# A four-stage Mamba, attention and experts model on one core: the experts' rounds written as one block, and decays, z, statistics and setup of the Mamba stage moved

## The reference, cut to what matters

```python
# step 1: four Mamba layers on x; per layer
xin, z = split(einsum('bld,ed->ble', layernorm(residual), in_w))   # 2 x 256 channels
u  = silu(causal_conv(xin, cw) + cb)                               # 4 taps
dtr, B, C = split(u @ xp_w.T)                                      # 8, 16, 16
dt = softplus(dtr @ dtp_w.T + dtp_b)
for n in range(16):                                                # states
    h[n] = exp(dt * A[n]) * h[n] + dt * u * B[n]                   # scan over the tokens
y  = (sum_n h[n] * C[n] + u * D) * silu(z)
hidden = y @ out_w.T
# step 2: cross-attention, 16 heads      step 3: experts (below)
# step 4: trajectory attention           step 5: top-k self-attention, cross-attention, ffn
# step 6: ternary-quantised gated ffn
# step 3: 8 heads choose 1 of 2048 experts each by product keys; their rows are gathered
lin = (x . A_in[idx]) * relu(score);  hid = gelu(x @ W_in.T + lin . B_in[idx])
out = hid @ W_out.T + ((hid . A_out[idx]) * gate) . B_out[idx]
```

## Time and profile before

| | us |
|---|---|
| median of 3 runs (lowest, highest) | 7854.28 (7828.51, 7878.61) |
| profiled execution, its span | 7862.71, 7860.9 |
| setup | 0 to 118 |
| Mamba stage | 118 to 3761 |
| cross-attention | 3761 to 4498 |
| experts | 4498 to 5514 |
| trajectory | 5514 to 5822 |
| decoder | 5822 to 7535 |
| last ffn | 7535 to 7861 |

### The profile page before, as it was taken

One profiled execution on the slowest core, in us unless ns is written; L12 is line 12 of the kernel. 1 busy time (PEld: TensorE's weight loads), 2 busy tenths in 40 slices (PEclk: granted clock), 3 DMA queues, 4 the chain that ended last, 5 costly groups with the idle time before them and its releaser, 6 DMA issues. The chain is left out here.

```text
span 7860.9 us, 92400 instructions
## 1 busy us (share of the span) xinstructions
PE 6285.0 (80%) x25986; PEld 3332.1 (42%) x26001; DVE 6331.9 (81%) x14154; ACT 4396.8 (56%) x8495; POOL 4934.3 (63%) x3020
## 2 busy tenths in 40 slices
PE   5888888988888988888798777777557777777745
PEld 2333333333333333333455545555334554545522
DVE  4999999999999999999555488888666666666557
ACT  3666666766666666766455434444225555555533
POOL 4999999998999989999322176666123444344300
PEclk9999999999999999999767788888557777777755
DMA  4444444444444444434101077776110000000011
GB/s 169 172 158 171 164 167 154 173 155 164 165 159 170 159 176 156 173 156 168 50 22 28 18 231 220 223 216 197 45 34 11 7 9 10 10 10 10 7 38 35
DMA packets 373862, 896.52 MB, mean 114 GB/s; under 512 B 28169, under 2 KB 270214, under 8 KB 307110
## 3 DMA queue, kind: packets, MB, share of 16 engines
q1 hardware_dynamic: 332646, 692.64, 24.0%
q0 software_dynamic: 40960, 201.36, 8.9%
HBM read 850.57 MB, written 56.77 MB: 115 GB/s over the span
## 5 line engine op out<-in xcount | busy, mean ns | idle before, releaser
L408 POOL TENSOR_TENSOR mb_dBu<-mb_dtu,mb_rows_b 128x1024 f32<-128x1024 f32 x1026 | 2398.5, 2362 | 74.5 <-DVE mb_bank L422 41.0
L422 DVE TENSOR_TENSOR_SCAN mb_bank<-mb_bank,mb_dBu 128x1024 f32<-128x1024 f32 x704 | 1608.7, 2285 | 92.5 <-PEq L594 49.6
L467 PE MATMUL mb_bank<-mb_hcd,ident 128*128 128x512 f32 x2560 | 1232.0, 612 | 105.9 <-DVE mb_hcd L439 98.9
L393 ACT ACTIVATE mb_bank<-mb_dt,mb_a_neg 128x508 f32<-128x508 f32 x2050 | 1311.1, 670 | 1.5
L450 POOL TENSOR_TENSOR mb_hcp<-mb_hs,mb_rows_c 128x1024 f32<-128x1024 f32 x320 | 753.5, 2355 | 221.4 <-DVE mb_hs L422 221.4
L439 DVE TENSOR_TENSOR mb_hcd<-mb_bank,mb_rows_c 128x1024 f32<-128x1024 f32 x704 | 861.8, 1224 | 31.4
L467 PEld LDWEIGHTS mb_bank<-mb_hcd,ident 128*128 128x128 f32 x2560 | 474.1, 195 | 758.8 <-issue 509.0
L422 DVE TENSOR_TENSOR_SCAN mb_hs<-mb_bank,mb_dBu 128x1024 f32<-128x1024 f32 x320 | 729.6, 2280 | 0.0
L1588 POOL DMA_INDIRECT ex_rows<-in_ex_table,ex_idx x512 | 492.0, 961 | 330.7 <-issue 169.0
L467 PE MATMUL mb_bank<-mb_hcp,ident 128*128 128x512 f32 x1024 | 544.9, 659 | 140.2 <-POOL mb_hcp L450 139.3
L390 ACT ACTIVATE mb_bank<-mb_zeros 128x8 f32<-128x8 f32 x1025 | 176.0, 172 | 755.5 <-DVE mb_hcd L439 330.2
(11 more groups left out here) (372 smaller groups left out, 12903.1 us busy)
## 6 DMA issues: line engine op xcount, KB each, us to landing
mb_rows_b<-bc_rows SPq DMA_DIRECT2D x259, 1024.0 KB, 7.0
mb_rows_c<-bc_rows SPq DMA_DIRECT2D x258, 1024.0 KB, 6.7
stream<-mb_r_post SPq DMA_DIRECT2D x69, 256.0 KB, 2.4
mb_r_tok<-stream SPq DMA_DIRECT2D x67, 256.0 KB, 2.7
mb_r_old<-stream SPq DMA_DIRECT2D x65, 256.0 KB, 2.8
ex_rows<-in_ex_table,ex_idx POOLq DMA_INDIRECT x512, 5.5
tj_x_tok<-stream SPq DMA_DIRECT2D x17, 256.0 KB, 3.0
bc_rows<-mb_xp SPq DMA_DIRECT2D x65, 64.0 KB, 2.1
```

What stands on the lines that cost most here:

```text
L393: e = nc.scalar.activation(da_of(n)[:, c * GB:(c + 1) * GB, 1:], dt[q][:, c].rearrange("p (b t) -> p b t", b=GB)[:, :, 1:], ACT.Exp, scale ...
L408: nc.gpsimd.tensor_tensor(by_c(dBu[m % RING][:]), by_c(chains(dtu[q][:])), over_c(rows_b[:, n]), ALU.mult).then_inc(s["mb_dbu"], 1)
L422: nc.vector.tensor_tensor_scan(flat(to), flat(da_of(n)), flat(dBu[n % RING][:]), 0.0, ALU.mult, ALU.add).then_inc(s["mb_scan"], 1)
L467: m = nc.tensor.matmul(bank[:, B_Y + c], ident[:], part[:, c * GB:(c + 1) * GB], start=(n == 0), stop=False)
```

## The change

- **Setup**: the copies are taken out of the first block. Four (`early`, 9.4 MB) are issued by SP in the fill block behind the weights, nine (`late`, 4.0 MB) behind its third load of tokens, and all are waited for at that block's end. The first layer reads x itself. Of the clears, those of the small constants stand at the fill block's start and four tiles' later, the PSUM banks' clear is replaced by matmuls of the identity with a zero tile.
- **Statistics**: in the rounds, the mean and the variance come from ACT, by four Copies and four Squares that also sum (`act_sums` at n = 14 of the round before, `act_squares` at n = 0), in place of DVE's two kinds of statistics at n = 3.
- **z**: on PE it stands ahead of the wait for yg and of sum(0).
- **Early decay**: da(4) is computed right behind da(3), ahead of the table load and the Silus, into an SBUF tile (ey) in place of PSUM, and scan 4 reads it there.
- **Layer weights**: skip, w_out, w_x, conv_b and norm_wb are made on ACT; w_u is first copied to PSUM by ACT, and DVE's four products read it there, at n = 12.
- **Turns**: in the attention, trajectory and decoder stages two sets of semaphores take turns, as in the Mamba stage; 53 clears with barrier go. The decoder loops over 6 pairs of rounds.
- **Experts**: the nine rounds become one straight block of 64 batches (and three steps of drain) without clears, barriers or branches.

```diff
@@ -35,6 +35,7 @@
 LATE = 2
+EARLY = 4
...
+        early_da = ey[:].rearrange("p c (b t) -> p (c b) t", b=GB)
...
-        with nc.Block() as block:
-            @block.vector
-            def _(dve):
-                nc.vector.memset(h_ch[:], 0.0)
...
-                nc.vector.memset(bank[:, B_DA:8], 0.0)
-
         s = Turns(nc, ctx, ["mb_" + n for n in [
...
+            def act_sums(self, act, there):
+                act.wait_ge(s["mb_res"], there)
+                for b in range(GB):
+                    m = nc.scalar.activation(xh[:, b], r_tok[:, b], ACT.Copy, accum_out=sums[:, b:b + 1])
+                m.then_inc(s["mb_sums"], 1)
+                act.wait_ge(s["mb_sums"], 1)
+                nc.scalar.activation(shift[:], sums[:], ACT.Copy, scale=-1.0 / D).then_inc(s["mb_mean"], 1)
+
+            def act_squares(self, act):
+                for b in range(GB):
+                    m = nc.scalar.activation(xh[:, b], r_tok[:, b], ACT.Square, bias=shift[:, b:b + 1],
+                                             accum_out=squares[:, b:b + 1])
+                m.then_inc(s["mb_squares"], 1)
+                act.wait_ge(s["mb_squares"], 1)
+                nc.scalar.activation(var[:], squares[:], ACT.Identity, bias=eps_at[:, 0:1], scale=1.0 / D).then_inc(s["mb_var"], 1)
...
                 q = self.q if m < DS else self.next_q
                 n = m % DS
-                if j >= 1:
+                if m == EARLY:
+                    pass
+                elif j >= 1:
                     if m - 2 in ON_POOL:
                         act.wait_ge(s["mb_scan"], m - 1)
                     else:
                         act.wait_ge(s["mb_hcd"], ON_VECTOR.index(m - 2) + 1)
                 if m == DS:
                     act.wait_ge(s["mb_dt"], 1)
-                nc.scalar.activation(da_of(n)[:, :, 0:1], zeros[:], ACT.Copy)
+                da = early_da if n == EARLY else da_of(n)
+                nc.scalar.activation(da[:, :, 0:1], zeros[:], ACT.Copy)
...
-                nc.vector.tensor_tensor_scan(flat(to), flat(da_of(n)), flat(dBu[n % RING][:]), 0.0,
+                da = early_da if n == EARLY else da_of(n)
+                nc.vector.tensor_tensor_scan(flat(to), flat(da), flat(dBu[n % RING][:]), 0.0,
...
-        def dve_weights(dve):
-            dve.wait_ge(s["mb_raw"], 5 * 16)
+        def dve_weights(dve, base):
             for k in range(DC):
-                nc.vector.tensor_tensor(w_conv[:, k, :], w_u[:], conv_row[:, k, :], ALU.mult)
...
+                m = nc.vector.tensor_tensor(w_conv[:, k, :], base, conv_row[:, k, :], ALU.mult)
+            m.then_inc(s["mb_wb"], 1)
+
+        def act_copies(act):
+            nc.scalar.activation(w_x[:], x_raw[:], ACT.Copy)
+            nc.scalar.activation(conv_b[:], vec[:, CB:CB + CH], ACT.Copy)
+            nc.scalar.activation(norm_wb[:], vec[:, NW:NW + 2], ACT.Copy).then_inc(s["mb_copies"], 1)
+            act.wait_ge(s["mb_copies"], 1)
+
+        def act_skip(act):
             for c in range(CH):
-                m = nc.vector.tensor_scalar(skip[:, c], ident[:], vec[:, DD + c:DD + c + 1], None, ALU.mult)
+                m = nc.scalar.activation(skip[:, c], ident[:], ACT.Copy, scale=vec[:, DD + c:DD + c + 1])
             m.then_inc(s["mb_skip"], 1)
 
         def act_a_pos(act):
...
-                pre.load(sp, 1)
+                pre.load(sp, x_in, 0)
                 load_raw(sp, 0)
                 load_used(sp, 0)
+                moves = early(sp, s["mb_moved"])
                 sp.wait_ge(s["mb_xh"], 1)
-                again.load(sp, 2)
+                again.load(sp, x_in, 1)
                 first.store_rows(sp)
                 for name in ("b0", "c0", "b1", "c1", "b2"):
                     fill.rows_of(sp, 0, name)
                 sp.wait_ge(s["mb_xh"], 2)
-                again.load(sp, 3)
+                again.load(sp, x_in, 2)
+                moves += late(sp, s["mb_moved"])
...
+                sp.wait_ge(s["mb_moved"], 16 * moves)
...
+                nc.vector.memset(h_ch[:, :, 0:DC - 1], 0.0)
...
                 dve.wait_ge(s["mb_res"], 16)
                 pre.dve(dve)
-                dve_weights(dve)
-                dve_skip(dve)
+                dve.wait_ge(s["mb_raw"], 5 * 16)
+                dve_weights(dve, w_u[:])
+                nc.vector.memset(hcd[HCD[-1]][:], 0.0)
+                nc.vector.memset(hcp[(len(ON_POOL) - 1 + 1) % 2][:], 0.0)
+                nc.vector.memset(zg[1][:], 0.0)
+                nc.vector.memset(w_out[:], 0.0).then_inc(s["mb_blank"], 1)
                 first.dve_poly(dve)
                 first.dve_log(dve)
...
-                        scan.act_da(act, n + 1, n)
+                        if n + 1 != EARLY:
+                            scan.act_da(act, n + 1, n)
                         if n == 2:
+                            scan.act_da(act, EARLY, n)
                             for c in range(CH):
                                 ahead.act_conv(act, c, 1)
                             act.wait_ge(s["mb_yg"], 1)
...
                         if n == 4:
                             ahead.act_x(act)
-                        if n == 5:
-                            pre.act_var(act)
+                        if n == 0:
+                            pre.act_squares(act)
+                        if n == 5 and shape == 0:
+                            act.wait_ge(s["mb_out"], 1)
+                            nc.scalar.activation(w_out[:], out_raw[:], ACT.Copy).then_inc(s["mb_wo"], 1)
+                            act_skip(act)
+                        if n == 9 and shape == GROUPS - 2:
+                            act.wait_ge(s["mb_raw"], 5 * 16)
+                            act.wait_ge(s["mb_xp"], 1)
+                            act_copies(act)
+                        if n == 11 and shape == GROUPS - 2:
+                            act.wait_ge(s["mb_dt"], 1)
+                            nc.scalar.activation(bank[:, M1, 0:DI], w_u[:], ACT.Copy).then_inc(s["mb_wu"], 1)
+                        if n == 14:
+                            pre.act_sums(act, 16)
                         if n == 6:
                             ahead.act_exp(act)
...
-                        if n == 6 and shape == 0:
-                            nc.vector.tensor_copy(w_out[:], out_raw[:]).then_inc(s["mb_wo"], 1)
-                        if n == 6 and shape == GROUPS - 2:
-                            dve.wait_ge(s["mb_xp"], 1)
-                            dve_weights(dve)
-                        if n == 6 and shape == 0:
-                            dve_skip(dve)
-                        if n == 3:
-                            pre.dve(dve)
+                        if n == 12 and shape == GROUPS - 2:
+                            dve.wait_ge(s["mb_wu"], 1)
+                            dve_weights(dve, bank[:, M1, 0:DI])
                         if n == 8:
...
                     behind.pe_late_sums(pe)
                     ahead.pe_conv(pe, 1)
+                    ahead.pe_z(pe)
                     pe.wait_ge(s["mb_yg"], 1)
                     scan.pe_sum(pe, 0)
-                    ahead.pe_z(pe)
                     scan.pe_sum(pe, 1)
                     ahead.pe_x(pe)
                     behind.pe_out(pe, True)
...
@@ xattn_stage, trajectory_stage, decoder_stage (the same in each)
-        s = Sems(nc, st, ["xa_" + n for n in [
+        s = Turns(nc, st, ["xa_" + n for n in [
...
+            s.use(shape % 2)
...
                 def _(sp):
+                    s.clear_other()
...
-            s.clear()
...
@@ experts_stage
-        def round_of(i, shape):
-
-
...
-        round_of(0, 0)
-        with nc.Fori(1, GROUPS // 2 - 1) as i:
-            round_of(i, 1)
-        round_of(GROUPS // 2 - 1, GROUPS // 2 - 1)
-        round_of(GROUPS // 2, GROUPS // 2)
+        r = Round(0)
+        ENDED = GB * GROUPS + 3
+        with nc.Block() as block:
+            @block.sync
+            def _(sp):
+                for g in range(GROUPS + 1):
+                    here, other = g % 2, (g - 1) % 2
+                    if g < GROUPS:
+                        if g >= 2:
+                            sp.wait_ge(p[f"stored{here}"], 16 * (g // 2))
+                        sp.dma_start(y_tok[here][:], tile_rows(x_in, g)).then_inc(p[f"r{here}"], 16)
+                    if g >= 1:
+                        sp.wait_ge(p[f"n{other}_rows"], (g - 1) // 2 + 1)
+                        sp.dma_start(tile_rows(x_out, g - 1), y_tok[other][:]).then_inc(p[f"stored{other}"], 16)
+                    if g + 2 < GROUPS:
+                        sp.wait_ge(p["lin"], GB * (g + 1))
+                        sp.dma_start(x_tok[here][:], tile_rows(x_in, g + 2)).then_inc(p[f"x{here}"], 16)
...
+            @block.vector
+            def _(dve):
+                for k in range(ENDED):
+                    if r.has(k):
+                        r.dve_inner(dve, k)
+                    if r.has(k - 1):
+                        r.dve_outer(dve, k - 1)
```

(32 more changed lines are left out.)

207 lines of the change are left out of this document (83 added, 124 removed).

## The result

The change made the kernel slower: 7929.6 us (median of 4 runs, 7918.9 to 7941.3) against 7853.8 before, a ratio of 1.0099 with a 95% interval of 1.0069 to 1.0128. The forecast was 7852, no change. The measured time lies 5 above the forecast's own bounds (7720 to 7925) and inside the wider range that takes in the near edges of the rivals (7700 to 7960). The move of 75.8 is clear of its interval, though it is less than the 79 that the prediction took as noise.

The account below looks back on a forecast made before the run. DVE was taken to set the pace, POOL close behind. From 7862.7, five gains of 167 (setup, weights, borders, jumps, experts) against +158 in the Mamba rounds gave 7853.7, put at 7852; own bounds 7720 to 7925, with rivals' near edges 7700 to 7960.

Parts of the forecast that it names:

- Setup: Before the first scan: fill block no longer waits for the HBM copies, round 0 starts near 69.5; -48.5 (-44 to -54).
- Layer weights: Mamba stage: DVE gives weight products to ACT and reads the remaining 16 from PSUM; -31 us (-28 to -33).
- steps (a) to (d): Mamba rounds: (a) statistics to ACT, (b) da(4) early, delaying u(0), (c) z before sum(0), (d) clock; +158 (+46 to +212).
- step (d): Mamba rounds: PE's new 3.6 us pause brings the 1.2 GHz clock in half the rounds; +54 (0 to +109).
- Step (c): Mamba rounds: z waits for u(0), PE idles 3.6, x starts 3.1 later, scan 6 waits; net +1.9 per round, +122.
- Later decays follow as just in time as before: Mamba rounds behind scan 6: no further waits of DVE on decays, costed at nothing.
- The rule on SBUF's port: Scan 4, reading two SBUF tiles, waits for POOL's product: 1.4 later, next product 2.3 later; forecast sum unchanged.
- Borders: Three stages' round borders: 53 clears with barrier go, -16 (-5 to -32); seven fewer decoder jumps, -16.5 (0 to -32).
- Experts: Experts stage: one straight block loses DVE's waits at the borders between rounds; -55 us (-49 to -60).
- the rival of the stalling block: Experts: straight block stalls on instruction supply at the same rate, only the last border gained; 7902, chance 0.06.
- the slower one: Rival: the clock falls after the pause before z in all 64 Mamba rounds; 8017, chance 0.12.
- The faster one: Rival: the chain to scan 6 does not bind, each Mamba round keeps its 1.23; 7599 or 7690, chance 0.14.

Follow-up runs that it names:

- sbuf_da: both_back with da(4) written to the SBUF tile, order unchanged, so that scan 4 reads two SBUF tiles: 7823.1 us, ratio 0.9985 to the kernel before.
- z_back: The changed kernel with z back behind sum(0) on PE, all else kept: 7758.0 us, ratio 0.9876 to the kernel before.
- both_back: The changed kernel with z back behind sum(0) and da(4) back in its old place in PSUM: 7718.8 us, ratio 0.9840 to the kernel before.
- early_off: The changed kernel with da(4) back behind z's Silu and in PSUM, z still ahead of sum(0): 7824.9 us, ratio 0.9962 to the kernel before.

## Why the prediction was right or wrong

**Setup** (-48.5): right in mechanism and in place. Of the miss of 3.7, 2.0 are the third load of tokens, issued at 56.6 in place of 54.6; the rest is not placed.

**Layer weights** (-31): -34.5 at scan 6 to 7 and +5.3 at 12 to 13, together -29. The products from PSUM took 0.41 each and, as they overlap, 5.6 for 16 (6 forecast).

**Rounds**, steps (a) to (d) (+158): the mechanism was right, and so was most of the sum. The ledger's places 3 to 6, in which these steps lie, went from 683.1 to 839.6, +156.5. Of that 47 are what the rounds at the low clock take over the steady 4.18 at 5 to 6; step (d) had 54. The rest is 1.71 a round, where steps (a) to (c) had 1.9 less the waits of the earlier trace rows. Part of this is luck. Step (c) wanted PE to idle 3.6 before z in every round, and it idled 1.8 in 34 rounds, since its walk started at full clock and did not have the late sums at the low one. Scan 6 came 4.18 behind scan 5 with either pause. In step (d) each pause from 3.3 on was to be followed by the low clock, as 8 of 8 had been; 22 of 29 were.

**A term put at nothing** failed beside it: "Later decays follow as just in time as before". The interval 9 to 10 grew by 18.6, 0.29 a round, and 1 to 2 by 4.2. With these the rounds cost +178 in place of +158.

**The rule on SBUF's port**: the trace agrees with the Trainium skill ("SBUF — State Buffer", "Who interferes with whom"): scan 4 takes 3.53 on average where the others take 2.29, 1.29 in a steady round against a forecast of 1.4, and POOL's five products 13.59 against 11.62. That it did not change the sum here, as forecast, is argued from the wait of scan 6; sbuf_da shows its price where nothing covers it: 104 in the medians, 115 in the stage. The prediction also had a scan 4 above 2.3 among its signs of being wrong, and named the port as the story then. The sign came, but z_back shows that the port was not the story.

**Statistics**: costed at nothing on ACT, right; a sum takes 0.29 and reading it 0.19, in ACT's idle time; the decays behind were not late for it, as both_back shows.

**Borders**: this step failed, and it is the largest part of the miss. The forecast was -16 for 53 clears and -16.5 for the decoder's jumps, at the least -5 together. In the changed kernel the three stages gave +2.6: trajectory -6.9, decoder -6.4 and cross-attention +15.9, and that against a profile of before that took 722 where its other one took 672. Giving the cross-attention its barriers back took 29 to 50 off the whole. The borders' waits did fall (from 53.5 to 46.2 on DVE), but PE sets the pace there (DVE waits 187.0 and 57.7 for its products), at a clock that is low half the time, and with shorter borders the rounds ran in a repeating pattern with more of it (mean clock 0.68 against 0.72 and 0.79). In the decoder 27 of waiting at borders went and 19 came back behind PE's matmuls. The same edits on the kernel before gave 18 of the 32.5, and their forecast share in trajectory and decoder. So what failed is that the gain would carry over to stages that run behind other ones; why it does not is open. The prediction's bounds for both terms came from DVE's idle time and left out that PE's clock could move in a stage whose clock averages 0.72: they should have had a loss at one end.

**Experts** (-55): -49.6, at the near end of the range of -49 to -60. A straight block is supplied: by the starts of the sums into ex_y_tok, taken at every eighth, eight batches take 112.6 to 113.7 (14.1 to 14.2 each, as forecast), where they took 118.1 to 121.6. So the rival of the stalling block is out. What came in place of a border is a wait for ACT's hidden layer, 8.7 in place of 1.1.

**Rivals**: the slower one had the right mechanism with a third of the rounds where it wanted all. The faster one (the chain does not bind) is out by z_back.

The misses, against the span, are: cross-attention +21 and decoder +16, which are the borders; rounds +20; experts +5, setup +4, weights +2, and the rest near 0. Together they are 68, which is 59.3 less the forecast's -9.

## What to carry to other kernels

Before an operation is moved forward on an in-order engine, look at what it waits for: z in front of sum(0) moved nothing forward, since Silu had to free its banks first, and put a pause of 1.8 us or more into PE's order, ahead of everything behind it. Work taken from the busiest engine is gained only up to the next operand that is late: of 79 us of statistics 13 at most were. Where TensorE sets the pace at a clock that falls and rises, a saved pause is not a saved time: measure it on its own, beside the other edits, and more than once. Here the best version, both_back with the later wait and with barriers in the cross-attention, runs at 7664.5 to 7684.5, 2.1 to 2.3% below before.

## What the runs showed of the hardware

- A scan with both inputs in SBUF beside POOL's products takes 3.5 to 3.9 us in place of 2.29. It ends 2.1 to 2.2 behind the end of the POOL product that ran at its start, in each of 64 rounds, and a product of POOL that falls on it takes 4.3 to 4.4 in place of 2.36.
- An ACT pass of 128x128 that also sums takes 0.29 (Copy) or 0.39 (Square), and each is followed by a read of the accumulator of 0.19 that occupies ACT.
- A pause of TensorE of 3.3 us or more before z was followed by the low clock in z in 22 of 29 rounds of the changed kernel, and one of 1.7 to 1.8 in none of 34. In early_off one of 2.0 to 2.1 was so in 18 of 37.
- The same program's cross-attention took 722 and 672 us in two executions with the same instructions, at mean granted clocks of 0.72 and 0.79. Without barriers and behind the changed Mamba rounds nine profiles lie within 10 us of each other, at 0.68 to 0.70.
